# Edge corrections of a style-modulated convolution chain: narrow column tiles replaced by wide stationary operands

## The reference

```python
def _layer(x, style, w, b, mw, mb, typ):
    s = style @ mw.T + mb                       # per-sample modulation
    weight = SCALE * w * s[:, None, :, None]
    demod = lax.rsqrt(jnp.sum(weight * weight, axis=(2, 3)) + EPS)
    weight = weight * demod[:, :, None, None]
    # 'same': conv, 3 taps;  'upsample': transposed conv, stride 2, then blur (1,3,3,1)
    # 'downsample': blur, then conv with stride 2
    ...
for i, typ in enumerate(('same', 'upsample', 'same', 'downsample')):
    out = _layer(out, style, weights[i], biases[i], mod_w[i], mod_b[i], typ)
```

## Time and profile before

| | |
|---|---|
| median of 3 runs | 1113.19 us (1113.07 to 1116.12) |
| profiled execution | 1112.61 us |
| its span in the trace | 1110.8 us |
| PE busy | 1069.1 us (96%) |
| DVE, ACT, POOL busy | 504.9, 331.3, 507.1 us |
| mean granted clock of PE | 0.994 of full speed |

### The profile page before, as it was taken

How to read it: one execution, slowest core, us unless ns; L and a number is a source line. 1 busy time by engine, 2 the same in 40 slices (tenths; PEclk the granted TensorE clock), 3 DMA queues, 4 the chain that set the end, 5 groups by cost and what they waited for, 6 DMA issues and landing times.

```text
span 1110.8 us, 47494 instructions
## 1 busy us (share of the span) xinstructions
PE 1069.1 (96%) x22064; PEld 794.4 (72%) x22064; DVE 504.9 (45%) x1244; ACT 331.3 (30%) x721; POOL 507.1 (46%) x380
## 2 busy tenths in 40 slices
PE   5899999999999999999999999999999999999997
PEld 4457777776777777777777777777777777777775
DVE  5774443543444344544343345544344345534353
ACT  2323323234322322323332224223222333323321
POOL 2536745345535552465435452655442543744500
PEclk9799999999999999999999999999999999999999
DMA  4535400002334200002123300002115200000211
GB/s 142 191 129 217 155 3 2 3 3 69 116 100 141 70 3 3 2 2 69 41 81 114 107 12 2 3 2 59 52 60 143 70 3 3 2 3 23 58 40 38
DMA packets 30084, 64.92 MB, mean 58 GB/s; under 512 B 5632, under 2 KB 6720, under 8 KB 27968
## 3 DMA queue, kind: packets, MB, share of 16 engines
q1 hardware_dynamic: 28352, 61.51, 17.7%
q10 hardware_dynamic: 1536, 0.39, 0.2%
HBM read 44.05 MB, written 17.83 MB: 56 GB/s over the span
## 4 chain that ended last, share of the span: by engine, by line
PE 84%; DVE 4%; ACT 2%; issue 1%; DVEq 0%
PE bank_b L1570 16%; PE bank_a L1570 15%; PE bank_a L108 10%; PE bank_b L108 10%; PE bank_a L91 5%; PE bank_b L91 5%; PE bank_b L79 3%; PE bank_a L79 3%; PE bank_a L67 2%; PE bank_b L67 2%; DVE y3t_lo L1313 2%; ACT y3t_hi L1184 2%; PE bank_b L1518 1%; PE bank_a L1518 1%; PE bank_a L1580 1%
## 5 line engine op out<-in xcount | busy, mean ns | idle before, releaser
L1131 POOL TENSOR_TENSOR xs<-x,tab 128x512 f32<-128x512 f32 x96 | 110.9, 1164 | 368.3 <-DVE x L1321 368.3
L1118 POOL TENSOR_TENSOR sums<-raw 128x896 f32<-128x896 f32 x62 | 128.3, 2090 | 35.2 <-ACT raw L1171 35.2
L108 PE MATMUL bank_a<-y,wv 32*64 32x256 f32 x4096 | 116.2, 375 | 0.5 <-issue 0.5
L108 PE MATMUL bank_b<-y,wv 32*64 32x256 f32 x4096 | 116.0, 375 | 0.1
L1570 PE MATMUL bank_b<-w_hi,y3t_hi 128*128 128x512 f32 x256 | 104.8, 409 | 3.9 <-ACT y3t_hi L1184 1.6
L1570 PE MATMUL bank_a<-w_hi,y3t_hi 128*128 128x512 f32 x256 | 104.7, 409 | 2.4 <-DVE y3t_lo L1313 1.1
L108 PEld LDWEIGHTS bank_a<-y,wv 32*64 32x64 f32 x4096 | 94.7, 130 | 15.1 <-issue 1.8
L108 PEld LDWEIGHTS bank_b<-y,wv 32*64 32x64 f32 x4096 | 93.9, 130 | 16.1 <-issue 1.9
L1570 PE MATMUL bank_b<-w_lo,y3t_hi 128*128 128x512 f32 x256 | 100.4, 392 | 0.0
L1570 PE MATMUL bank_a<-w_lo,y3t_hi 128*128 128x512 f32 x256 | 100.4, 392 | 0.0
L1321 DVE TENSOR_TENSOR x<-bank_a,x 128x512 f32<-128x512 f32 x64 | 43.5, 690 | 102.9 <-PE bank_a L1570 75.3
(11 more groups left out here) (297 smaller groups left out, 1868.3 us busy)
## 6 DMA issues: line engine op xcount, KB each, us to landing
w_hi<-w_scratch SPq DMA_DIRECT2D x36, 256.0 KB, 3.2
w_lo<-w_scratch SPq DMA_DIRECT2D x36, 256.0 KB, 3.2
x_in<-in_x SPq DMA_DIRECT2D x32, 256.0 KB, 4.6
out_x<-x SPq DMA_DIRECT2D x32, 256.0 KB, 2.4
w_raw<-in_w SPq DMA_DIRECT2D x3, 1024.0 KB, 9.0
w_scratch<-w_hi SPq DMA_DIRECT2D x3, 1024.0 KB, 4.1
w_scratch<-w_lo SPq DMA_DIRECT2D x3, 1024.0 KB, 7.0
w_raw<-w_scratch SPq DMA_DIRECT2D x2, 1024.0 KB, 10.4
```

What stands on the lines that cost most here:

```text
L108: last = pe.matmul(banks[b][2 * CH * h:2 * CH * (h + 1), HALF * u:HALF * (u + 1)], keep["wv"][rows, a, SPAN - q:SPAN - q + 2].rearrange("p ...
L1118: g_.tensor_tensor(sums[i][:], pairs[:, :, one[0], one[1]:one[1] + SPAN], pairs[:, :, other[0], other[1]:other[1] + SPAN], ALU.add).then_i ...
L1131: nc.gpsimd.tensor_tensor(xs[:, b, 1:LEN + 1], src[:, b], column(n, T_S, b).broadcast_to((P, LEN)), ALU.mult).then_inc(xs_ready, 1)
```

## The change

The three strips of `edge_1` become one matmul with a stationary operand of 96 columns, plus the accumulated one of 32 columns; `edge_2` becomes one of 96 columns for each end; `edge_3` takes both parities as one operand of 64 columns. A phase has 4 + 2 + 4 = 10 edge matmuls instead of 8 + 6 + 8 = 22. For `edge_3` the layout of `down_e` is swapped in its last rows, in the setup program.

```diff
     for e in range(2):
-        for k in range(3):
-            to = out[CH * k:CH * (k + 1), e]
-            last = pe.matmul(to, keep["up_e"][:, l, e, k], keep["y0_e"][:, e, e].rearrange("p b a -> p (b a)"),
-                             start=True, stop=(k < 2), skip_group_check=True)
-            if k == 2:
-                last = pe.matmul(to, keep["up_e"][:, l, e, 0], keep["y0_e"][:, e, 1 - e].rearrange("p b a -> p (b a)"),
-                                 start=False, stop=True, skip_group_check=True)
+        pe.matmul(out[:, e], keep["up_e"][:, l, e].rearrange("p k o -> p (k o)"),
+                  keep["y0_e"][:, e, e].rearrange("p b a -> p (b a)"), start=True, stop=False, skip_group_check=True)
+        last = pe.matmul(out[2 * CH:STACK, e], keep["up_e"][:, l, e, 0],
+                         keep["y0_e"][:, e, 1 - e].rearrange("p b a -> p (b a)"),
+                         start=False, stop=True, skip_group_check=True)
 ...
 def edge_2(pe, bank, keep, l):
     for e in range(2):
-        for k in range(3):
-            last = pe.matmul(out[CH * k:CH * (k + 1), e], keep["w2_e"][0:STACK, l, e, k], keep["b_e"][0:STACK, e],
-                             start=True, stop=True, skip_group_check=True)
+        last = pe.matmul(out[:, e], keep["w2_e"][0:STACK, l, e].rearrange("p k o -> p (k o)"), keep["b_e"][0:STACK, e],
+                         start=True, stop=True, skip_group_check=True)
 ...
 def edge_3(pe, bank, keep, l):
-    for h in range(2):
-        for parity in range(2):
-            at = CH * (2 * h + parity)
-            for e in range(2):
-                last = pe.matmul(out[at:at + CH, e], keep["down_e"][0:STACK, l, parity, e],
-                                 keep["c_e"][0:STACK, e].rearrange("p (b u h) -> p h u b", u=2, h=2)[:, h],
-                                 start=True, stop=True, skip_group_check=True)
+    for e in range(2):
+        for h in range(2):
+            at = 2 * CH * h
+            last = pe.matmul(out[at:at + 2 * CH, e], keep["down_e"][0:STACK, l, e].rearrange("p y o -> p (y o)"),
+                             keep["c_e"][0:STACK, e].rearrange("p (b u h) -> p h u b", u=2, h=2)[:, h],
+                             start=True, stop=True, skip_group_check=True)
 ...
-            a.activation(down_e[rows, :, 1, 0], d6[rows, :, BLURRED - 1], ACT.Copy)
-            a.activation(down_e[rows, :, 0, 1], d6[rows, :, 0], ACT.Copy).then_inc(down_ready, 1)
+            a.activation(down_e[rows, :, 0, 1], d6[rows, :, BLURRED - 1], ACT.Copy)
+            a.activation(down_e[rows, :, 1, 0], d6[rows, :, 0], ACT.Copy).then_inc(down_ready, 1)
```

## The result

The changed kernel is slower: 1124.47 us median of 5 runs (1123.86 to 1126.28) against 1113.19 (1112.66 to 1116.12, 5 runs). The ratio is 1.010, 95% interval 1.0086 to 1.0114, so +9.6 to +12.7 us. The forecast was 1127.6, range 1114 to 1134, and the measured time lies inside.

What follows compares the result with a forecast made beforehand. PE was taken to bound the kernel: +0.44 us a phase over 31 phases made +13.6, setup +0.8, total +14.4 on 1112.61 us, so 1127.0, plus 0.6 for the median: 1127.6 us, range 1114 to 1134.

Steps and rivals of the forecast that it cites:

- What bounds the kernel: Main program: PE, busy for 96% of the span, so a stage's time on PE is paid in full unless in waits.
- The change of shape: Edge stages on PE: a new array shape starts at last start + length - 0.07 us, 0.113 behind a 16-column matmul.
- The loads: Weight loads on PE cost by columns, 0.81 ns each; wide operands were taken as spaced 0.083 us apart.
- The strip with eight instructions: edge_1 before: one strip carries 8 of 16 instructions one after another, 8 x 0.031 = 0.25 us; other strips were free.
- The sum: Per phase: edge_1 +0.34, edge_2 +0.03, edge_3 +0.07, together +0.44 us; 31 phases +13.6, total with setup +14.4.
- Setup's +0.8: Setup program, one set more: edge_1 loses as elsewhere and edge_2 now has to change shape, estimated +0.8 us.
- A: Edge stages bound by instruction count, 20 instead of 44: faster, -0.50 us a phase, 1098 us; chance 0.10.
- B: Inside edge_1, turns between 96 and 32 columns are free: +0.13 us a phase, 1117.5 us; chance 0.11.
- C: Whole kernel: no measurable change, with loads hidden but turns paid, 1114 us; chance 0.07.

Runs made afterwards that it cites:

- e1_grouped: Changed kernel with both wide matmuls of edge_1 ahead of both narrow ones, reference's result not computed: 1122.15 us, ratio 1.0083 against the kernel before.
- four_strips: Kernel before, with edge_1's product of the other parity on a fourth strip and summed by edge_2: 1107.77 us, ratio 0.9962.
- nofar_narrow: Kernel before without edge_1's product of the other parity, leaving 12 narrow instructions: 1108.15 us, ratio 0.9957.
- all_wide: Changed kernel with edge_1's product of the other parity also 96 columns wide, 64 of them zero: 1122.22 us, ratio 1.0090 against the kernel before.
- nofar_wide: Changed kernel without edge_1's product of the other parity, leaving two wide matmuls: 1112.53 us, ratio 0.9991 against the kernel before.
- e1_wide: Kernel before with only edge_1 made wide, 96 and 32 columns in turn: 1127.72 us, ratio 1.0126.
- e23_wide: Kernel before with only edge_2 and edge_3 made wide, including the layout of down_e: 1117.78 us, ratio 1.0037.

## Why the prediction held

*What bounds the kernel.* Right: PE's stages are paid in full, and other engines kept their busy times.

*The change of shape.* Right in sign and size. At each boundary of the timeline after, the next shape starts 0.06 to 0.07 us before the modelled end of the last: 531.20 against 531.13, 531.36 against 531.30, 531.64 against 531.57, 531.80 against 531.74. This doesn't go with the length of the old one. Between 100 and 1080 us of the trace before there are 320 changes of shape (96 rows or columns counted as 128), behind matmuls 0.18 to 0.59 us long. In 306 of them the new shape starts 0.07 us before the last modelled end, in the other 14 later, in none earlier. In one shape a start that comes before that end is at least 0.09 us ahead of it, in the median 0.37. That PE finishes first is read from this and from no other record. By the rule of the prediction (last start + length - 0.07) `edge_1` came to 1.03 us, and is 1.03. Grouped, it came to 0.82 and is 0.82. That 96 columns belong to the shape of 128 is shown by the entries of 0.23, and that 64 are a shape of their own by the entry of `edge_3` after the change, 0.32 us from 541.38 (540.70 + 1.07 - 0.39) to 541.70:

```profile
540.70 1.07 PE L1566 MATMUL bank_a<-w_hi,y3t_lo 128*128 128x512 f32 x4
541.70 0.41 PE L140 MATMUL bank_a<-c_e,down_e 96*64 96x8 f32 x8
```

*The loads.* Right: the wide spacing was taken as 0.083 us and is 0.085, for 96 columns that have no strip beside them. The 96-column load of line 119 lasts 161 ns in the median, one of 64 columns (line 140) 138 and one of 32 (line 121) 108 to 109. One detail was wrong without weight in the sum: behind the base the second wide instruction is recorded 0.03 after the first, not 0.08, but it is longer, 0.236 us against the 0.183 of a narrow one, and by the rows of the weight loads that is its load: the load runs from 530.95 to 531.11, the matmul's record from 530.97 to 531.20. The row of line 119 in one bank (duration ns min/median/max):

```profile
L119 PE MATMUL bank_a<-y_e,up_e x64: 177/236/257, 136.3 to 1077.3; 128*96 128x16 f32 x64
```

The two cancel: 0.03 + 0.236 - 0.07 is 0.20, and 0.083 + 0.113 was 0.196.

*The strip with eight instructions.* The prediction named it as what bounds `edge_1` before, 8 x 0.031 us; `four_strips` and `nofar_narrow` show it, since each takes four instructions off that strip and the stage falls from 0.37 to 0.25 and 0.24. Both also take away the accumulation on top of the third strip, so that is a rival; against it, wide instructions start 0.085 us apart with accumulation (`all_wide`) and without it (`nofar_wide`).

*The sum.* Per phase, from the rows: `edge_1` +0.34 as forecast, `edge_2` +0.03 to +0.04 (forecast +0.03), `edge_3` +0.06 to +0.07 (forecast +0.07), so +0.44, and the median phase grew by 0.45. In the 8 phases where line 1518 stands before `edge_2`, its change costs nothing: 1.03 us to the next start with its entry, before and after. 31 phases make 13.6 us. Between the two profiled executions the span did grow by 13.7 us, but that match is luck. The first instruction of phase 1 starts at 94.14 us instead of 92.17:

```profile
94.14 1.44 PE L91 MATMUL bank_a<-xs,cw 32*32 32x512 f32 x33 [0.49 <-PEq L281]
```

So 2.0 us arise in setup and 11.7 behind it. The 11.7 hold two things that happened once and nearly cancel. The kernel before had the long wait for `y0_e`, 1.4 us more than the kernel after. And the last phase of the kernel after grew by 1.75 us instead of 0.45: PE's granted clock fell there, behind a wait of 2.6 us that the kernel before has as well. This is the stretch from 1100 to 1105 us, where the kernel before has a clock of 1.00:

```profile
1100.00:1105.00 5.00, 3.72 (x18) 0.66 0.00 0
```

By the rows and these two (13.6 - 1.4 + 1.3) it would be 13.5 us. The 1.8 us that are missing lie for the most part in stages that the change doesn't touch, 1.5 us in the span, whose matmuls of line 108 are busy for 232.2 us before and 230.7 after in all. What stretches single spans in one execution and not in the next was not found. In the medians the growth is 11.3 us (9.6 to 12.7), so the forecast of +14.4 is high by 1.7 to 4.8; where that goes in executions without a trace is open.

Setup's +0.8 can't be read from these two executions, since the clock differs: between 40 and 60 us 0.83 was granted before and 0.75 after, which alone is about 1.6 us by my estimate (20 us x 0.08). Four other traces had the same clock there (1.00 up to 40 us, 0.91 from 40 to 60). Phase 1 starts at 91.33 us in `four_strips`, whose stages are narrow, at 91.96 in `nofar_wide`, and at 92.25 and 92.33 in `e1_grouped` and `all_wide`. So wide stages cost 0.6 to 1.0 us in setup, near the +0.8; the changed kernel itself has no trace at that clock.

*The rivals.* A, a price for each instruction, is refuted by `four_strips` (same number, faster) and by the result itself. B, free changes of shape inside `edge_1`, is refuted by the rows and by `e1_grouped` (same instructions, two changes fewer, 0.2 us less). C needed wide loads at 0.031 us; they take 0.085.

## What to carry to other kernels

Before merging small matmuls into one with a wider stationary operand, look at which matmuls stand around it: in this kernel the matmul behind a change of the array's shape started no earlier than 0.07 us before the modelled end of the last one (0.32 us behind the start of a 512-column matmul instead of 0.23, and 0.11 behind that of a narrow 16-column one instead of 0.03), and in `edge_1` a merged operand of 96 columns beside one of 32 bought three such changes inside, and saved one on entry, for eight instructions less: 1.03 us instead of 0.69. In `edge_1`, wide operands alone were shorter than narrow ones only where matmuls of 128 columns stood on both sides (0.52 us against 0.57, and 0.59 against 0.56 before taps). Matmuls on different column strips loaded their weights side by side: before the change the 16 loads of `edge_3`, 110 ns each, lie within 0.24 us (535.13 to 535.37), four on each strip. So count the instructions on the fullest strip, not all of them. Where one strip carries twice the load of the others, spread it, and let a later contraction do the addition: eight instructions on one strip took 0.37 us to the next stage, four on each of four 0.25.

## What the runs showed of the hardware beyond that

The start of the kernel differs from one execution to the next by microseconds, and PE's granted clock differs with it: in the three executions below phase 1 starts at 92.17, 94.14 and 97.07 us, of which the wide stages explain at most 1.0. Each row has a stretch, PE's busy time, the granted clock, and transfers; first the kernel before, then after, then `e1_wide`:

```profile
45.00:55.00 10.00, 10.00 (x106) 0.90 0.01 2
75.00:85.00 10.00, 10.00 (x136) 1.00 0.82 290
```

```profile
45.00:55.00 10.00, 10.00 (x86) 0.75 0.00 0
75.00:85.00 10.00, 10.00 (x146) 1.00 0.64 226
```

```profile
45.00:55.00 10.00, 10.00 (x90) 0.74 0.01 2
75.00:85.00 10.00, 10.00 (x62) 0.70 0.69 246
```

The mean of 0.74 in `e1_wide` is made of two halves, 0.50 from 45 to 50 us and 0.97 from 50 to 55:

```profile
45.00:50.00 5.00, 5.00 (x64) 0.50 0.02 3
50.00:55.00 5.00, 5.00 (x27) 0.97 0.00 0
```

PE was busy for the whole stretch in all three, and what it did before hardly differs: in the 10 us before, it was busy for 6.03, 5.83 and 6.04 us, at 0.76, 0.74 and 0.75. The clock also fell in the main program, behind a wait. In `e1_wide` it did so 2.1 us behind the wait of 1.7 us for `y0_e` that ended at 205.16 us:

```profile
205.00:210.00 5.00, 4.84 (x31) 0.73 0.01 3
```

PE was granted 1.00 from 205 to 207 us and 0.50 from 207.3 to 210.

The phase with both was 3.4 us longer than in the kernel before, of which the wide `edge_1` explains 0.3. Behind setup this execution was 15.2 us longer, where the rows of `edge_1` explain 31 x 0.34 = 10.5. The profiled execution of `e1_wide` was its slowest, 1132.73 us, with a mean clock of 0.988, while its two fastest, 1123.04 and 1123.22 us, had 0.995 and 0.994. So a comparison of two single executions of this kernel can be off by several microseconds that no edit caused; the kernel before alone took 1109.64 to 1117.30 us in 20 runs. Whether the wide operands themselves make the low clock likelier is left open: `nofar_wide` and `e23_wide`, both with wide operands, had mean clocks of 0.991 to 0.998 and 0.990 to 0.997, the kernel before 0.991 to 0.998.
